# Two attention layers on one core: where the second layer keeps its scaled scores, and which engine hands a pair of score banks back

## Chip, cores and metric

One Trainium2 chip, one of its cores. The metric is the device time of one execution in microseconds (us). Engines are named as in the profile: PE (TensorE; its weight loads are listed as PEld), DVE (VectorE), ACT (ScalarE), POOL (GpSimd), SP (SyncE, which issues the transfers).

## What is computed

Two self-attention layers over 8 images of 64 x 64 positions with 64 channels, all in float32:

```python
xf = x.reshape(8, 4096, 64)
# layer 0
f = xf @ wf + bf            # 8 columns
g = xf @ wg + bg            # 8 columns
hh = xf @ wh + bh           # 64 columns
attn = softmax(einsum('bnk,bmk->bnm', g, f))
x1 = gamma0 * einsum('bnm,bmc->bnc', attn, hh) + xf
# layer 1
q = x1 @ Wq + bq;  k = x1 @ Wk + bk;  v = x1 @ Wv + bv      # 64 columns each
attn = softmax(einsum('bic,bjc->bij', q, k))
out = gamma1 * einsum('bmn,bmc->bnc', attn, v) + x1
```

In layer 1 the second product contracts over m, the index along which the rows of the softmax run: out[n] is the sum over m of attn[m, n] v[m]. So a tile with 128 values of m in its partitions and n along its columns can be used as it is, and the factor 1/(sum of row m) can be put into v[m].

## The kernel before

The program is written by hand: each engine has its own list of instructions, and semaphores hold them together. It runs through the 8 images, and for each first through layer 0 and then through layer 1 (in the code `chunk0` and `steps1`). Layer 0 is not touched by the change.

**Layer 1.** An image has T = 32 blocks of 128 queries, and each block has NCH = 4 chunks of CH = 1024 keys. One step is one chunk of one block, so a block of queries is four steps, j = 0 to 3, and an image has 128 steps. The code counts u = 0 to 7 over two blocks of queries. The steps go through four kinds of work:

- PE, `scores1` (L559 to L569): the 128 x 1024 scores of step u, into one of two pairs of PSUM banks, the pair u % 2 of `score_banks`. Queries and keys are split into float16 parts, so each half (512 columns, h = 0 and 1) takes matmuls with `k_high` and with `k_low`, two each. `s_ready` tells DVE that both halves are there.
- DVE (L1088 to L1091), called the minimum below: one instruction multiplies the 1024 scores by `neg_down` and keeps the smallest product, which is minus the largest score of each row in this chunk. It goes to `exp_bias[:, u]`. The products themselves go to a scratch tile, `scaled`, a view of `o_tr`, which nobody reads. `bias_ready` counts it.
- ACT (L811 to L819): two exponentials of 512 columns, each from one PSUM bank into `e_whole[:, u]`, with `exp_bias[:, u]` as bias and `down` as scale, and with the sum of the row in `part_sum`. `exp1_done` counts them.
- PE, `values1` (L571 to L581): seven steps later (LAG1 = 7), the slot `e_whole[:, u]` times `v_scaled[:, ..., j]` is added to `sum_banks[:, j]`. `pv1_done` counts it. `e_whole` has eight slots.

Each chunk of a row has a maximum of its own, so the row needs weights. After j = 3 DVE takes the smallest `exp_bias` of the four chunks (`neg_row1`, L1094), ACT makes four weights (`chunk_w`, L823), and in the next block of queries DVE works out from them and from `part_sum` the sum of the row and its reciprocal (`weigh_chunks`, L1061 to L1071, behind the minimum of j = 1), and then multiplies the values of the block (`weigh_values`, L1073 to L1082, behind the minimum of j = 2, written to `v_scaled`). The first `values1` of a block of queries waits for `v_scaled_ready`; PE reaches it in step j = 3 of the next block.

**Who hands a pair of banks back.** Both DVE and ACT read a bank, ACT last. So `scores1` waits, for each half by itself, for ACT's exponential of the same half two steps before:

```python
for h in range(2):
    pe.wait_ge(exp1_done, 2 * (image * STEPS1 + k) + h + 1)
```

`credit` instructions of POOL at the start (L301 to L305) put a first number on such semaphores, so that the first steps find free slots (FREE_S1, FREE_E1).

POOL is idle in most of layer 1. In blocks 8 and 9 of each image it lays out `f_stack` and `g_stack` for the image after the next (L326, L330) and adds a bias (L335). In the first two blocks of queries PE, ACT and DVE also do the projections of the same image (L415, L407) and those of a later one (L387, L397, L761).

## Time and profile before

| | |
|---|---|
| median of 3 runs | 4228.95 us (4221.15 to 4231.31) |
| the profiled execution's own time | 4228.57 us |
| its span | 4226.4 us |
| PE busy | 4030.3 us (95%) |
| DVE busy | 3271.2 us (77%) |
| ACT busy | 3191.0 us (76%) |
| POOL busy | 1953.5 us (46%) |
| granted PE clock, mean | 0.972 of full speed |
| chain that ended last | PE 84%, DVE 6%, issue 6%, ACT 3% |
| its largest lines | L480 23% (layer 0), L578 20% and L566 20% (layer 1), L466 12% (layer 0) |
| transfers | 41.88 MB, 2.9% of the 16 engines' time |

Shares are of the span. A matmul is listed from its start to its modelled end, and matmuls overlap, so the pace of PE is read from the distance between starts and not from durations. The chain of waits is followed back from the last instruction. In the timeline a bracket gives how long the engine was idle before a row, and who released it.

### The profile page before, as it was taken

Reading aid. Unit: us, or ns where it says so; the run is one execution under the profiler, and the core shown is the slowest. Engines: PE = TensorE matmul, PEld = TensorE weight load, DVE = VectorE, ACT = ScalarE, POOL = GpSimd, SP = SyncE. Lnnn points to the kernel's source line nnn. Section 1 sums busy time; section 2 is a strip of 40 time slices with the busy share of each in tenths; the row PEclk is TensorE's granted clock in tenths of the full one; section 3 lists DMA queues with packets and bytes.
Section 4 is the critical chain, followed back from the end, with each engine's and each line's share of the span. In section 5 each row is a group of like instructions: output and inputs, shape, how many; then the busy total and the mean of one; then the engine's idle time right before and its main releaser. Section 6 shows DMA issues by size and latency. Waiting matters only on the chain.

```text
span 4226.4 us, 84183 instructions
## 1 busy us (share of the span) xinstructions
PE 4030.3 (95%) x25681; PEld 1349.5 (32%) x25681; DVE 3271.2 (77%) x6298; ACT 3191.0 (76%) x5674; POOL 1953.5 (46%) x909
## 2 busy tenths in 40 slices
PE   4999999999999999999999999999999999999999
PEld 3223332233322333223332233323333233322333
DVE  3877887778877787777877788777887778877787
ACT  2466896778867788767986689776897678977788
POOL 3596106941089311992029910497105961079410
PEclk7799999999999999999999999999999999999999
DMA  1001000010000000000000000001000010000000
GB/s 33 1 1 31 1 1 11 1 31 1 1 12 11 21 1 11 1 11 21 1 12 1 18 14 1 11 1 31 1 1 12 1 31 1 1 11 3 30 1 11
DMA packets 15060, 41.88 MB, mean 10 GB/s; under 512 B 4068, under 2 KB 4068, under 8 KB 12260
## 3 DMA queue, kind: packets, MB, share of 16 engines
q1 hardware_dynamic: 14692, 36.96, 2.9%
q8 instruction: 233, 3.82, 0.4%
q14 instruction: 135, 1.11, 0.1%
HBM read 20.17 MB, written 8.39 MB: 7 GB/s over the span
## 4 chain that ended last, share of the span: by engine, by line
PE 84%; DVE 6%; issue 6%; ACT 3%; POOL 0%; SPq 0%; DVEq 0%; DMA 0%; ACTq 0%; POOLq 0%
PE sum_banks L480 23%; PE sum_banks L578 20%; PE score_banks L566 20%; PE score_banks L466 12%; PE sum_banks L502 3%; PE sum_banks L438 2%; DVE tile_max L922 1%; DVE o_tr L1089 1%; ACT e_whole L816 1%; PE score_banks L430 1%; DVE c_stack L949 1%; ACT g_tr L734 1%; PE sum_banks L415 1%; DVE k_low L969 0%; DVE x_mid L1140 0%
## 5 line engine op out<-in xcount | busy, mean ns | idle before, releaser
L816 ACT ACTIVATE e_whole<-score_banks,exp_bias,down 128x512 f32<-128x512 f32 x2048 | 1573.9, 773 | 249.8 <-DVE o_tr L1089 211.3
L922 DVE TENSOR_REDUCE tile_max<-sum_banks 128x1 f32<-128x512 f32 (+1 forms) x2128 | 1364.8, 685 | 444.0 <-PE sum_banks L438 440.5
L355 POOL TENSOR_TENSOR e_sum<-e_sum,e_whole 128x1024 f32<-128x1024 f32 x704 | 1659.5, 2357 | 83.0 <-ACT e_whole L752 31.9
L752 ACT ACTIVATE e_whole<-score_banks,no_bias,down 128x1024 f32<-128x1024 f32 x1024 | 1229.0, 1204 | 527.1 <-PE score_banks L466 516.1
L1089 DVE TENSOR_SCALAR_CACHE_REDUCE o_tr<-score_banks,neg_down 128x1024 f32<-128x1024 f32 x1024 | 1313.6, 1283 | 320.4 <-PE score_banks L566 281.4
L480 PE MATMUL sum_banks<-e_whole,proj 128*64 128x512 f32 x4096 | 1123.3, 626 | 0.0
L578 PE MATMUL sum_banks<-e_whole,v_scaled 128*64 128x512 f32 x4096 | 1066.7, 602 | 45.1 <-DVE v_scaled L1079 17.1
L566 PE MATMUL score_banks<-k_high,q_split 128*64 128x512 f16 x4096 | 810.2, 388 | 30.6 <-ACT e_whole L816 9.7
L566 PE MATMUL score_banks<-k_low,q_split 128*64 128x512 f16 x4096 | 799.2, 382 | 0.0
L438 PE MATMUL sum_banks<-f_tr,g_tr 33*128 33x512 f16 x2128 | 700.4, 402 | 19.0 <-DVE tile_max L922 14.6
L352 POOL TENSOR_TENSOR e_sum<-e_whole 128x1024 f32<-128x1024 f32 x32 | 75.4, 2357 | 1355.5 <-ACT e_whole L752 1355.5
L466 PE MATMUL score_banks<-g_tr,f_tr 34*128 34x512 f16 x2048 | 644.2, 392 | 23.7 <-ACT g_tr L734 8.7
L566 PEld LDWEIGHTS score_banks<-k_high,q_split 128*64 128x64 f16 x4096 | 228.0, 107 | 753.2 <-ACT e_whole L816 716.1
L816 ACT ACTIVATION_READ_ACCUMULATOR e_whole<-score_banks,exp_bias,down 128x1 f32 x2048 | 398.2, 194 | 0.0
L578 PEld LDWEIGHTS sum_banks<-e_whole,v_scaled 128*64 128x64 f32 x4096 | 276.7, 137 | 309.2 <-issue 145.9
L466 PEld LDWEIGHTS score_banks<-g_tr,f_tr 34*128 34x128 f16 x2048 | 120.9, 94 | 744.9 <-issue 609.6
L566 PEld LDWEIGHTS score_banks<-k_low,q_split 128*64 128x64 f16 x4096 | 242.6, 111 | 208.0 <-issue 192.6
L480 PEld LDWEIGHTS sum_banks<-e_whole,proj 128*64 128x64 f32 x4096 | 206.2, 136 | 289.2 <-ACT e_whole L752 158.0
L438 PEld LDWEIGHTS sum_banks<-f_tr,g_tr 33*128 33x128 f16 x2128 | 178.6, 94 | 182.1 <-DVE tile_max L922 102.8
L502 PE MATMUL sum_banks<-e_whole,ones_w 128*32 128x256 f32 x2048 | 164.5, 393 | 0.0
L326 POOL TENSOR_TENSOR f_stack<-fg_high,ones_h 128x512 f16<-128x512 f16 x20 | 21.3, 1077 | 258.7 <-issue 250.4
L316 POOL PARTITION_ALL_REDUCE fg_top<-fg_abs x10 | 3.7, 372 | 257.5 <-issue 257.5
(147 smaller groups left out, 1868.5 us busy)
## 6 DMA issues: line engine op xcount, KB each, us to landing
x_in<-in_x_dram SPq DMA_DIRECT2D x19, 1024.0 KB, 4.9
out_dram<-x_mid SPq DMA_DIRECT2D x32, 256.0 KB, 2.7
k_high<-k_high SPq DMA_DIRECT2D x32, 128.0 KB, 2.2
k_low<-k_low SPq DMA_DIRECT2D x32, 128.0 KB, 2.2
w<-in_L_conv_wg_dram SPq DMA_DIRECT2D x2, 2.0 KB
w<-in_L_conv_wf_dram SPq DMA_DIRECT2D x2, 2.0 KB
w<-in_L_conv_wh_dram SPq DMA_DIRECT2D x2, 16.0 KB
b<-in_L_conv_bh_dram SPq DMA_DIRECT2D x1, 32.0 KB
```

The source lines that it names most:

```text
L352: nc.gpsimd.tensor_tensor(acc, e_whole[:, 0, :], e_whole[:, 1, :], ALU.add).then_inc(e_added, 1)
L355: nc.gpsimd.tensor_tensor(acc, acc, e_whole[:, i % U0, :], ALU.add).then_inc(e_added, 1)
L438: nc.tensor.matmul(sum_banks[:, (2 + j % banks) % 4, :], g_tr[HIGH:KX, par, q * CH + blk * P:q * CH + (blk + 1) * P], f_tr[HIGH:KX, par, j ...
L466: mm = nc.tensor.matmul(score_banks[:, 2 * (i % 2) + h, :], f_tr[0:KM, par, i * P:(i + 1) * P], g_tr[0:KM, par, q * CH + h * BANK:q * CH + ...
L480: mm = nc.tensor.matmul(sum_banks[half * C:(half + 1) * C, 0, :], proj[:, par, i, GFW:PW], e_whole[:, i % U0, half * BANK:(half + 1) * BAN ...
L502: mm = nc.tensor.matmul(sum_banks[rows, 1, 0:SQ], ones_w[:, :], terms[:, c * SQ:(c + 1) * SQ], start=first, stop=final, skip_group_check=True)
L566: mm = nc.tensor.matmul(bank[c * C:(c + 1) * C, :], q_split[:, query_col(i) + c * C:query_col(i) + (c + 1) * C], k_part[:, col:col + BANK] ...
L578: mm = nc.tensor.matmul(sum_banks[half * C:(half + 1) * C, j, :], v_scaled[:, u // NCH, j, :], half_of_chunk(u, half), start=i == 0, stop= ...
L752: nc.scalar.activation(e_whole[:, i % U0, :].rearrange("p (a n) -> p a n", a=2), score_banks[:, 2 * (i % 2):2 * (i % 2) + 2, :], ACT.Exp, ...
L816: nc.scalar.activation(e_whole[:, u, h * BANK:(h + 1) * BANK], score_banks[:, 2 * (u % 2) + h, :], ACT.Exp, bias=exp_bias[:, u:u + 1], sca ...
L922: nc.vector.reduce_max(tile_max[:, blk, j:j + 1], sum_banks[:, (2 + j % banks) % 4, :], AX_X).then_inc(a_used, 1)
L1089: nc.vector.tensor_scalar(scaled[:, u % 2, :], score_banks[:, 2 * (u % 2):2 * (u % 2) + 2, :] .rearrange("p a n -> p (a n)"), neg_down[:, ...
```

## The change

In layer 1 the minimum writes its products into the slot of the probabilities, `e_whole[:, u]`, in place of the scratch tile. It therefore waits for `pv1_done` as well, which tells that the slot's last content has been used. ACT then makes one exponential of 1024 columns in place in that slot, with scale -1.0, and no longer reads PSUM; it waits for `bias_ready` alone. `part_sum` has one sum per chunk and not two. `scores1` waits for `bias_ready`, that is for DVE's minimum two steps before, once for both halves. The credit of two slots moves from `exp1_done` to `bias_ready`. `weigh_values` comes right behind `weigh_chunks` at j = 1. `down` is no longer made.

```diff
-    FREE_ST, FREE_A, FREE_E0, FREE_S1, FREE_E1 = 2, 4, U0, 4, U1
+    FREE_ST, FREE_A, FREE_E0, FREE_S1, FREE_E1 = 2, 4, U0, 2, U1
...
-            nc.gpsimd.memset(credit[:, 3:4], 0.0).then_inc(exp1_done, FREE_S1)
+            nc.gpsimd.memset(credit[:, 3:4], 0.0).then_inc(bias_ready, FREE_S1)
...
             def scores1(image, i, k, u):
+                pe.wait_ge(bias_ready, image * STEPS1 + k + 1)
                 for h in range(2):
-                    pe.wait_ge(exp1_done, 2 * (image * STEPS1 + k) + h + 1)
...
-                pe.wait_ge(exp1_done, 2 * (image * STEPS1 + t * U1 + u + 1) + FREE_S1)
+                pe.wait_ge(exp1_done, image * STEPS1 + t * U1 + u + 1)
...
-                        act.wait_ge(bias_ready, step + 1)
-                        act.wait_ge(pv1_done, step + 1)
-                        for h in range(2):
-                            nc.scalar.activation(e_whole[:, u, h * BANK:(h + 1) * BANK], score_banks[:, 2 * (u % 2) + h, :],
-                                                 ACT.Exp, bias=exp_bias[:, u:u + 1], scale=down[:, par:par + 1],
-                                                 accum_out=part_sum[:, u // NCH, u % NCH, h:h + 1]
-                                                 ).then_inc(exp1_done, 1)
+                        act.wait_ge(bias_ready, step + 1 + FREE_S1)
+                        nc.scalar.activation(e_whole[:, u, :], e_whole[:, u, :], ACT.Exp, bias=exp_bias[:, u:u + 1],
+                                             scale=-1.0, accum_out=part_sum[:, u // NCH, u % NCH:u % NCH + 1]
+                                             ).then_inc(exp1_done, 1)
...
-                    dve.wait_ge(exp1_done, 2 * (image * STEPS1 + (i + 1) * NCH) + FREE_S1)
+                    dve.wait_ge(exp1_done, image * STEPS1 + (i + 1) * NCH)
...
                         dve.wait_ge(s_ready, k + 1)
-                        nc.vector.tensor_scalar(scaled[:, u % 2, :], score_banks[:, 2 * (u % 2):2 * (u % 2) + 2, :]
+                        dve.wait_ge(pv1_done, k + 1)
+                        nc.vector.tensor_scalar(e_whole[:, u, :], score_banks[:, 2 * (u % 2):2 * (u % 2) + 2, :]
...
                             if j == 1:
                                 weigh_chunks(t * 2 + odd - 1, 1 - odd)
-                            elif j == 2:
                                 weigh_values(t * 2 + odd - 1, 1 - odd)
```

**DVE's order.** Behind the minimum of j = 1 in the loop over blocks of queries, before: `part_scr` to `norm_w` are `weigh_chunks`, `v_scaled` is `weigh_values`, ISA and REGISTER_ALU are the sequencer's own.

```order
L1065 ISA part_scr,row_sum<-part_sum,chunk_w 128x8 [waits exp1_done]
L1065 ISA row_sum 128x1
L861 ISA
L1069 RECIPROCAL inv_sum<-row_sum 128x1 [waits dve_step]
L861 REGISTER_ALU
L1070 TENSOR_SCALAR norm_w<-chunk_w,inv_sum 128x4 [waits dve_step]
L1088 REGISTER_ALU
L1089 TENSOR_SCALAR o_tr,exp_bias<-score_banks,neg_down 128x1024 [waits s_ready]
L1077 REGISTER_ALU [waits dve_step]
L1078 ISA [waits v1_biased]
L1079 ISA [waits pv1_done]
L1079 TENSOR_TENSOR v_scaled<-v,norm_w 128x256
```

and of the changed kernel, at the same place:

```order
L1058 ISA part_scr,row_sum<-part_sum,chunk_w 128x4 [waits exp1_done]
L1058 ISA row_sum 128x1
L856 ISA
L1061 RECIPROCAL inv_sum<-row_sum 128x1 [waits dve_step]
L856 REGISTER_ALU
L1062 TENSOR_SCALAR norm_w<-chunk_w,inv_sum 128x4 [waits dve_step]
L1069 REGISTER_ALU [waits dve_step]
L1070 ISA [waits v1_biased]
L1071 ISA [waits pv1_done]
L1071 TENSOR_TENSOR v_scaled<-v,norm_w 128x256
L1080 REGISTER_ALU
L1082 TENSOR_SCALAR e_whole,exp_bias<-score_banks,neg_down 128x1024 [waits pv1_done,s_ready]
```

The product for `v_scaled` now stands between the minima of j = 1 and j = 2, right behind `norm_w`, and no longer between those of j = 2 and j = 3.

**PE's order.** One step of `scores1` with the `values1` in front of it, before:

```order
L578 MATMUL sum_banks<-e_whole,v_scaled 64x512 [waits exp1_done]
L578 MATMUL sum_banks<-e_whole,v_scaled 64x512
L561 ISA
L566 MATMUL score_banks<-k_high,q_split 64x512 [waits exp1_done]
L566 MATMUL score_banks<-k_high,q_split 64x512
L566 MATMUL score_banks<-k_low,q_split 64x512 x2
L561 REGISTER_ALU
L566 MATMUL score_banks<-k_high,q_split 64x512 [waits exp1_done]
L566 MATMUL score_banks<-k_high,q_split 64x512
L566 MATMUL score_banks<-k_low,q_split 64x512 x2
```

and of the changed kernel:

```order
L576 MATMUL sum_banks<-e_whole,v_scaled 64x512 [waits exp1_done]
L576 MATMUL sum_banks<-e_whole,v_scaled 64x512
L558 REGISTER_ALU
L564 MATMUL score_banks<-k_high,q_split 64x512 [waits bias_ready]
L564 MATMUL score_banks<-k_high,q_split 64x512
L564 MATMUL score_banks<-k_low,q_split 64x512 x2
L564 MATMUL score_banks<-k_high,q_split 64x512 x2
L564 MATMUL score_banks<-k_low,q_split 64x512 x2
```

The matmuls are the same; two waits on ACT's count have become one on DVE's.

## Rows read from the trace of the kernel before

**Rows 1.** The page, part 1: busy time, share of the span, instructions.

```profile
PE 4030.3 (95%) x25681; PEld 1349.5 (32%) x25681; DVE 3271.2 (77%) x6298; ACT 3191.0 (76%) x5674; POOL 1953.5 (46%) x909
```

**Rows 2.** Windows of image 1's layer 1: length, busy per engine, granted clock.

```profile
969.00:988.00 19.00, 15.53 (x100) 5.42 (x98) 17.19 (x31) 13.91 (x37) 13.21 (x9) 1.00 0.00 1
988.00:1150.00 162.00, 159.49 (x1054) 59.28 (x1050) 134.06 (x308) 146.17 (x373) 0.00 (x0) 1.00 0.00 1
```

**Rows 3.** Waits, 988 to 1150 us: total us, times, longest.

```profile
PEld score_banks L566 <- ACT e_whole L816: 60.7, 175, 0.6
```

**Rows 4.** One line's instructions, 990 to 1151 us: ns min/median/max, first and last start.

```profile
L1079 DVE TENSOR_TENSOR v_scaled<-v,norm_w x22: 421/422/422, 994.1 to 1149.8; 128x256 f32<-128x256 f32 x22
```

**Rows 5.** Timeline, image 0, PE's two gaps in a block: start, us.

```profile
504.32 0.39 PE L566 MATMUL score_banks<-k_low,q_split 128*64 128x512 f16 x2
504.50 0.20 ACT L816 ACTIVATION_READ_ACCUMULATOR e_whole<-score_banks,exp_bias,down 128x1 f32 x1
...
504.74 0.41 PE L566 MATMUL score_banks<-k_high,q_split 128*64 128x512 f16 x2
...
506.62 0.42 DVE L1079 TENSOR_TENSOR v_scaled<-v,norm_w 128x256 f32<-128x256 f32 x1
506.71 0.38 PE L566 MATMUL score_banks<-k_low,q_split 128*64 128x512 f16 x2
...
507.17 1.08 PE L578 MATMUL sum_banks<-e_whole,v_scaled 128*64 128x512 f32 x4
...
508.94 1.03 PE L578 MATMUL sum_banks<-e_whole,v_scaled 128*64 128x512 f32 x4
...
510.66 1.03 PE L578 MATMUL sum_banks<-e_whole,v_scaled 128*64 128x512 f32 x4
```

**Rows 6.** Timeline, same block: from scores through DVE's minimum to the next minimum.

```profile
502.38 0.39 PE L566 MATMUL score_banks<-k_high,q_split 128*64 128x512 f16 x2
...
503.46 1.28 DVE L1089 TENSOR_SCALAR_CACHE_REDUCE o_tr<-score_banks,neg_down 128x1024 f32<-128x1024 f32 x1 [0.43 <-PE score_banks L566]
...
504.67 0.08 DVE L1089 DVE_READ_ACCUMULATOR o_tr<-score_banks,neg_down 128x1 f32 x1
504.67 0.16 DVE L1065 CUSTOM_DVE_ANT_1 part_scr<-part_sum,chunk_w 128x8 f32<-128x8 f32 x1
...
505.07 0.23 DVE L1070 TENSOR_SCALAR norm_w<-chunk_w,inv_sum 128x4 f32<-128x4 f32 x1
...
505.41 1.28 DVE L1089 TENSOR_SCALAR_CACHE_REDUCE o_tr<-score_banks,neg_down 128x1024 f32<-128x1024 f32 x1
...
507.13 1.28 DVE L1089 TENSOR_SCALAR_CACHE_REDUCE o_tr<-score_banks,neg_down 128x1024 f32<-128x1024 f32 x1
...
508.46 0.16 DVE L1094 TENSOR_REDUCE neg_row<-exp_bias 128x1 f32<-128x4 f32 x1
```

**Rows 7.** Groups by line and form: busy, mean ns of one, idle before.

```profile
L816 ACT ACTIVATE e_whole<-score_banks,exp_bias,down 128x512 f32<-128x512 f32 x2048 | 1573.9, 773 | 249.8 <-DVE o_tr L1089 211.3
...
L752 ACT ACTIVATE e_whole<-score_banks,no_bias,down 128x1024 f32<-128x1024 f32 x1024 | 1229.0, 1204 | 527.1 <-PE score_banks L466 516.1 <-POOL e_sum L355 9.7
...
L823 ACT ACTIVATE chunk_w<-exp_bias,neg_row 128x4 f32<-128x4 f32 x256 | 74.2, 290 | 0.0
```

**Rows 8.** Timeline of DVE in image 1, beside POOL's work in block 8.

```profile
974.35 1.27 DVE L1089 TENSOR_SCALAR_CACHE_REDUCE o_tr<-score_banks,neg_down 128x1024 f32<-128x1024 f32 x1
...
975.55 0.79 DVE L1065 CUSTOM_DVE_ANT_1 part_scr<-part_sum,chunk_w 128x8 f32<-128x8 f32 x1
...
978.46 1.13 DVE L1079 TENSOR_TENSOR v_scaled<-v,norm_w 128x256 f32<-128x256 f32 x1
```

**Rows 9.** Timeline of DVE in block 2: an operation of layer 0's between two minima.

```profile
926.99 0.69 DVE L985 TENSOR_TENSOR proj<-proj,b 128x512 f32<-128x512 f32 x1
927.83 1.28 DVE L1089 TENSOR_SCALAR_CACHE_REDUCE o_tr<-score_banks,neg_down 128x1024 f32<-128x1024 f32 x1
```

**Rows 10.** Timeline of PE in the first two blocks of image 1.

```profile
917.90 1.12 PE L397 MATMUL sum_banks<-w,x_tr 64*128 64x80 f32 x16 [0.74 <-ACT proj L761]
```

More of the change, by code:

```diff
@@ L155, in attention_pair_kernel @@
         up = sb("up", [P, 1], F32)
-        down = sb("down", [P, 2], F32)
         neg_down = sb("neg_down", [P, 2], F32)
@@ L160, in attention_pair_kernel @@
         chunk_w = sb("chunk_w", [P, 2, NCH], F32)
-        part_sum = sb("part_sum", [P, 2, NCH, 2], F32)
-        part_scr = sb("part_scr", [P, NCH, 2], F32)
+        part_sum = sb("part_sum", [P, 2, NCH], F32)
+        part_scr = sb("part_scr", [P, NCH], F32)
         row_sum1 = sb("row_sum1", [P, 2], F32)
@@ L201, in loads @@
             return image + 1 if early else image * 2
-        scaled = o_tr[:, :, :].rearrange("p (b a) n -> p b (a n)", b=2)
         g_cols = g_tr[:, :, :].rearrange("k a n -> k (a n)")
@@ L524, in chunk0 @@
                 if q == 0:
-                    pe.wait_ge(exp1_done, 2 * image * STEPS1 + FREE_S1)
+                    pe.wait_ge(bias_ready, image * STEPS1 + FREE_S1)
                     pe.wait_ge(h_biased, image + 1)
@@ L709, in image_steps @@
                 for n in range(4):
-                    pe.wait_ge(exp1_done, 2 * (image + 1) * STEPS1 - (2 if n < 2 else 0) + FREE_S1)
+                    pe.wait_ge(bias_ready, (image + 1) * STEPS1 - (1 if n < 2 else 0) + FREE_S1)
                     turn_stack(n, score_banks[:, n, :])
@@ L911, in scales @@
                 chain.link(nc.vector.tensor_scalar(up[:, :], inv_pow2[:, :], 2.0 ** HALF_TOP, None, ALU.mult))
-                nc.vector.scalar_tensor_tensor(down[:, par:par + 1], pow2[:, :], 2.0 ** (-2 * HALF_TOP), pow2[:, :],
-                                               ALU.mult, ALU.mult)
                 nc.vector.scalar_tensor_tensor(neg_down[:, par:par + 1], pow2[:, :], -2.0 ** (-2 * HALF_TOP), pow2[:, :],
@@ L1063, in weigh_chunks @@
                     dve.wait_ge(chunk_w_ready, image * T + i + 1)
-                    dve.wait_ge(exp1_done, 2 * (image * STEPS1 + (i + 1) * NCH) + FREE_S1)
+                    dve.wait_ge(exp1_done, image * STEPS1 + (i + 1) * NCH)
                     chain.link(nc.vector.tensor_tensor_reduce(
-                        out=part_scr[:, :, :], in0=part_sum[:, par, :, :],
-                        in1=chunk_w[:, par, :].unsqueeze(2).to_broadcast([P, NCH, 2]), scale=1.0, scalar=0.0,
+                        out=part_scr[:, :], in0=part_sum[:, par, :], in1=chunk_w[:, par, :], scale=1.0, scalar=0.0,
                         op0=ALU.mult, op1=ALU.add, accum_out=row_sum1[:, par:par + 1]))
@@ L1092, in steps1 @@
                         if j == NCH - 1:
-                            dve.wait_ge(bias_ready, k + 1)
+                            dve.wait_ge(bias_ready, k + 1 + FREE_S1)
                             nc.vector.tensor_reduce(neg_row1[:, odd:odd + 1], exp_bias[:, odd * NCH:(odd + 1) * NCH],
```

## The prediction

> **What bounds the kernel now.** I read the page's busy shares first: PE is busy for 95% of the span, DVE 77%, ACT 76% [rows 1]. But PE's durations overlap, so this does not say that PE is at its pace, and it mixes two layers. The change touches layer 1 alone, so I took windows of it. In the quiet part of an image, 988 to 1150 us, DVE is busy 134.06 of 162 us and ACT 146.17 (90%), at the full granted clock, 2.4 GHz [rows 2]. Then one line by its starts: `v_scaled` is made once per block of queries, and its 22 starts lie (1149.8 - 994.1) / 21 = 7.41 us apart [rows 4]. What PE could do is read where it runs without a gap: two `values1` starts with one step between them lie 510.66 - 508.94 = 1.72 us apart [rows 5], so four steps are 6.88 us. PE loses 7.41 - 6.88 = 0.53 us in each block of queries.
>
> The timeline shows where. First gap: a pair of matmuls normally follows the last by 1.72 / 8 = 0.215 us, but between 504.32 and 504.74 lie 0.42 us, and the later one starts 0.04 us behind ACT's readout (504.50 + 0.20) [rows 5]: 0.20 us lost, because the bank's half is held by the exponential. The waits agree: ACT is named 175 times in 162 us as releaser of the scores' weight loads [rows 3]; most of these are short and hidden, since the load comes ahead of its matmul. Second gap: `values1` starts at 507.17, 0.46 us behind the last scores pair at 506.71, and `v_scaled` ended at 506.62 + 0.42 = 507.04 [rows 5]: 0.25 us lost, waiting for DVE's product, which stands behind the minimum of j = 2. The rest, 0.08 us, is slower restarting behind the two. So layer 1 is bound by PE with two gaps, one made by ACT, one by the order on DVE. The change aims at both.
>
> **The change part by part.** All times below count from T, the start of the scores of step j = 1.
>
> *The banks come back from DVE.* DVE's minimum starts 503.46 - 502.38 = 1.08 us behind the start of its scores, the next operation follows 1.21 us after it (504.67), and its result is out after 1.29 us (504.67 + 0.08) [rows 6]. PE then follows 0.04 us later. In a plain step the pair is free at 1.08 + 1.29 + 0.04 = 2.41 us, and PE wants it after two steps, 3.44 us. First gap gone, with 1.03 us to spare.
>
> *The weights' work comes together.* Behind the minimum of j = 1 DVE now does all of it. Its length W: from `part_scr` to the end of `norm_w`, 505.07 + 0.23 - 504.67 = 0.63 us; `v_scaled` to the next minimum, 507.13 - 506.62 = 0.51 us [rows 5, 6]; and between them a wait for `norm_w` and two more instructions of the sequencer, which no row of before shows in this place. At least they cost nothing; at most, three times the 0.11 us between `norm_w`'s end (505.30) and the next minimum (505.41), where one such instruction stands [rows 6]: 0.33 us. I take that upper value, since the three come one after the other with nothing to hide them, so W = 1.47 us (1.14 at least). The minimum of j = 2 then ends for PE at T + 1.08 + 1.21 + W + 1.29 + 0.04 = T + 3.62 + W = T + 5.09. PE wants that pair after three steps, T + 5.16. It fits by 0.07 us, up to W = 1.54. This is the tight place of the change. Behind it, the whole load of DVE per block is 4 x 1.21 + 1.47 + 0.28 for `neg_row1` (508.46 + 0.16 - 507.13 - 1.21 [rows 6]) = 6.59 us, under 6.88. `v_scaled` is ready at T + 1.08 + 1.21 + 1.47 - 0.09 = T + 3.67, and PE wants it behind the scores of j = 3, at T + 3.44 + 0.86 = T + 4.30: second gap gone.
>
> *ACT's exponential.* Two of 773 ns become one of 1024 columns from SBUF, which no row shows. Lower bound: `chunk_w`, also from SBUF and with one pointer operand, takes 290 ns at 4 columns, and a column costs (1204 - 773) / 512 = 0.84 ns [rows 7], so 290 + 859 = 1.15 us. Upper: 1.204 us as L752, with the 0.20 us readout wholly behind it, 1.40 us [rows 5, 7]. I take the upper one; nothing hangs on it: 4 x 1.40 + 0.29 = 5.89 us per block, under 6.88. `values1` needs it seven steps later. `chunk_w` matters more, since `weigh_chunks` waits for it in front of the minimum of j = 2: by the same walk the exponentials of j = 2 and 3 end at T + 6.49 and T + 7.89 and the weights at T + 8.18, and DVE asks at T + 6.88 + 2.29 = T + 9.17. One microsecond to spare.
>
> The Trainium skill (VectorE: DVE Perf Modes, section "The TRN2 errata — SBUF-src ops pay a fixed extra latency per instruction") speaks against this step: ACT pays 224 fixed cycles from SBUF and 172 from PSUM. An estimate from that page is 0.04 us per exponential, 44 us over 1024 of them if ACT set the pace, and nothing in the sum as long as it does not; no row of before has the same exponential from both memories.
>
> *The minimum's new wait.* It waits for `pv1_done` of the slot's last use. PE has done that product one step before it sends the scores that the same minimum waits for, so it costs nothing. The dropped `down`, the halved `part_sum` and the one wait fewer per step on PE: nothing, off the path or hidden behind matmuls.
>
> *The sum, per image.* An image has 32 blocks of queries; the first two are filled with other work.
> - 30 blocks by 0.53 us by 8 images: 127 us.
> - In some four blocks of an image DVE has one more operation in front of the minimum of j = 1. L985 takes 927.83 - 926.99 = 0.84 us there [rows 9]. From the minimum of j = 0 the walk is 1.08 + 1.21 + 0.84 + 1.21 + 1.47 + 1.33 = 7.14 us against 6.88, so 0.26 us late; others are shorter. I take 0.2: 4 x 0.2 x 8 = 6 us given back (0 to 8).
> - Blocks 8 and 9, beside POOL: DVE's small operations grow, `part_scr` to 0.79 and `v_scaled` to 1.13 us [rows 8], and in 19 us PE is idle for 3.47 [rows 2]. These operations come all the same, so most of the stall stays. Between nothing and 1.1 us more per image; I take 0.6, 5 us in all.
> - The first two blocks: one of PE's waits there is for ACT's copy of the projections (917.90, 0.74 us) [rows 10], and ACT is less loaded; their other waits I leave as they are. Between 0 and 2.5 us; I take 0.9 by the one row, 7 us in all.
> - The end of the layer is PE's own chain of products and transposes: nothing. Layer 0: nothing.
>
> 127 - 6 + 5 + 7 = 133 us. The profiled execution took 4228.6 us itself (the median of the runs is 4228.95, the same), so 4096 us.
>
> **The rivals.**
>
> *DVE's bundle is too long.* The block then takes 1.72 + 3.62 + W = 5.34 + W. At W = 1.84, 0.1 us more for each of the three sequencer instructions and a late start, it takes 7.18, 0.30 more than in the forecast: 240 blocks by 0.30 = 72 us, so 4168 us; 4115 to 4190 for what lies around it. For it: only 0.07 us to spare. Against: W is already at its upper bound.
>
> *The release is not what holds PE.* If `chunk_w` came late, DVE would stand in front of the minimum of j = 2 and PE behind it, and the chain would again run over ACT. It needs more than 1 us of delay over two exponentials, so about 1.9 us each instead of 1.40. The old pace is reached at (7.41 - 0.29) / 4 = 1.78 us per exponential. Then 4229 less the start, 4222 to 4230. Against: 1.204 us from PSUM. The rule on SBUF sources would make 1.44.
>
> *Slower: the minimum pays for its new place.* It now writes into the tile that ACT reads and writes and PE streams from, where before it had a scratch tile to itself. With d more per minimum DVE's load is 6.59 + 4d; it passes the old 7.41 us at d = 0.21. At d = 0.3 a block takes 7.79, 0.38 more than before: 240 by 0.38 = 91 us, so 4320 us. For it: small DVE operations grow fourfold beside POOL. Against: the minimum itself takes 1.27 us even there [rows 8], and L816 has written to that tile while PE read it all along.
>
> **How the numbers follow.** The forecast has 0.76 (4065 to 4115: the low end adds 1.1 and 2.5 us per image for the two bounded terms and leaves the 6 us out, 4072, and a little for what I don't see), the too long bundle 0.15, no change 0.05, slower 0.04. The range 4065 to 4145 leaves out the far half of the second case and the last two. About 13 us (0.3%) is what can be told from no change. Faster 0.91, same 0.05, slower 0.04.
>
> **What would show it.** The starts of `v_scaled` 6.88 us apart in the quiet part; ACT gone as releaser of the scores' weight loads; `values1` of j = 0 without a wait for `v_scaled`; one exponential of 1.15 to 1.2 us per step and ACT's busy time in layer 1 down by a quarter; DVE's minimum still at 1.28 us; between `norm_w` and `v_scaled` at most 0.33 us. I am wrong if the blocks stay above 7.0 us: with DVE named in front of the scores of j = 0 it was the bundle, with ACT in front of `part_scr` it was the weights, with the minimum above 1.4 us it was the new place.

## The result, and the profile after

The changed kernel takes 4096.85 us (median of 4 runs, 4095.08 to 4101.33); the kernel before, on the same chip, 4225.3 us (4221.15 to 4231.31). The ratio is 0.9697, with a 95% interval of 0.9681 to 0.9712: 3% faster, 128 us. The forecast was 4096.0 us. The profiled execution has a span of 4094.2 us and a mean granted clock of 0.973, against 4226.4 us and 0.972 before.

The page of the changed kernel, part 1, which answers to [rows 1], and from its part 5 the two groups of layer 1 that replace the minimum and the exponentials of [rows 7] (busy us and mean ns of one, then idle time before and its releaser):

```profile
PE 3912.5 (96%) x25681; PEld 1450.7 (35%) x25681; DVE 3265.9 (80%) x6288; ACT 2789.5 (68%) x3626; POOL 1951.2 (48%) x909
...
L812 ACT ACTIVATE e_whole<-e_whole,exp_bias 128x1024 f32<-128x1024 f32 x1024 | 1176.1, 1149 | 518.4 <-DVE e_whole L1082 500.8
...
L1082 DVE TENSOR_SCALAR_CACHE_REDUCE e_whole<-score_banks,neg_down 128x1024 f32<-128x1024 f32 x1024 | 1292.8, 1281 | 132.0 <-PE score_banks L564 122.3
```

DVE's busy time is the same as before, ACT's is 402 us less. The minimum takes 1.281 us (1.283 before), so its new place costs it nothing. The exponential takes 1.149 us, exactly the lower bound of the prediction, which left the readout of the sum out; where two exponentials follow each other in the timeline, the second starts 1.20 us behind the first (500.57 and 501.77 in image 0).

Windows of image 1's layer 1, with the columns of [rows 2]: the first blocks of queries up to block 7 (905 to 949), blocks 8 and 9 beside POOL (949 to 968), and the quiet part:

```profile
905.00:949.00 44.00, 44.00 (x310) 23.62 (x308) 40.77 (x96) 32.12 (x59) 0.38 (x2) 1.00 0.01 1
949.00:968.00 19.00, 15.71 (x96) 6.22 (x94) 17.28 (x29) 10.05 (x19) 12.90 (x9) 0.91 0.01 2
968.00:1116.00 148.00, 148.00 (x1036) 64.63 (x1034) 129.47 (x302) 109.61 (x193) 0.00 (x0) 1.00 0.00 1
```

In the first and the last of them PE is busy all the time. ACT was busy 90% of its window before and is now busy 109.61 / 148 = 74%. Beside POOL the picture is another one: PE is idle for 3.29 of 19 us, as before (3.47), and the mean granted clock is 0.91 there.

The line that gave the pace in [rows 4], here from 968 to 1116 us:

```profile
L1071 DVE TENSOR_TENSOR v_scaled<-v,norm_w x22: 424/426/427, 970.5 to 1115.0; 128x256 f32<-128x256 f32 x22
```

(1115.0 - 970.5) / 21 = 6.88 us per block of queries, PE's own pace. The waits of the same stretch (total us, times, longest), for comparison with [rows 3]:

```profile
ACT e_whole L812 <- DVE e_whole L1082: 37.7, 44, 1.3
PEld score_banks L564 <- issue: 35.0, 119, 0.3
PEld score_banks L564 <- DVE e_whole L1082: 15.8, 42, 0.5
```

ACT, named 175 times before as releaser of the scores' weight loads, is gone from that place. DVE is named 42 times for at most 0.5 us, all of it hidden, since PE itself is never idle. The chain that ended last shows the same thing at the place where [rows 5] showed two gaps (start us, us, group). It now runs on PE alone, and a step takes 1.72 us, two rows of 0.86:

```profile
500.22 0.86 PE sum_banks L576 x4
501.08 0.86 PE score_banks L564 x8
501.94 0.86 PE sum_banks L576 x4
502.80 0.86 PE score_banks L564 x8
503.66 0.86 PE sum_banks L576 x4
```

Last, the tight place of the change: the timeline of DVE from `part_scr` to the next minimum, in two blocks that follow each other (image 0).

```profile
504.92 0.16 DVE L1058 CUSTOM_DVE_ANT_0 part_scr<-part_sum,chunk_w 128x4 f32<-128x4 f32 x1
...
505.31 0.23 DVE L1062 TENSOR_SCALAR norm_w<-chunk_w,inv_sum 128x4 f32<-128x4 f32 x1
505.94 0.42 DVE L1071 TENSOR_TENSOR v_scaled<-v,norm_w 128x256 f32<-128x256 f32 x1 [0.39 <-DVE norm_w L1062]
506.28 1.28 DVE L1082 TENSOR_SCALAR_CACHE_REDUCE e_whole<-score_banks,neg_down 128x1024 f32<-128x1024 f32 x1
...
511.80 0.16 DVE L1058 CUSTOM_DVE_ANT_0 part_scr<-part_sum,chunk_w 128x4 f32<-128x4 f32 x1
...
512.20 0.23 DVE L1062 TENSOR_SCALAR norm_w<-chunk_w,inv_sum 128x4 f32<-128x4 f32 x1
512.68 0.43 DVE L1071 TENSOR_TENSOR v_scaled<-v,norm_w 128x256 f32<-128x256 f32 x1 [0.25 <-DVE norm_w L1062]
513.02 1.28 DVE L1082 TENSOR_SCALAR_CACHE_REDUCE e_whole<-score_banks,neg_down 128x1024 f32<-128x1024 f32 x1
```

The length W is 506.28 - 504.92 = 1.36 us in one block and 513.02 - 511.80 = 1.22 us in the next, 1.29 on average, where the prediction had 1.47.

**Where the 128 us come from.** From the first to the last scores of an image, layer 1 took 250.5 us before and takes 234.0 now (means of the 8 images); the rest of an image, layer 0, takes 259.5 and 259.3. So all of it is layer 1: 16.5 x 8 = 132 us, which is the difference of the two profiled spans; the medians differ by 128. By the starts of DVE's minima, summed over the 8 images:

| blocks of queries of an image | before | after | difference | forecast |
|---|---|---|---|---|
| 0 and 1 (with layer 0's leftovers) | 188.0 | 177.8 | -10.2 | -7 |
| 2 to 7 (some with one more operation) | 359.3 | 330.6 | -28.7 | -19 (25 less 6) |
| 8 to 10 (beside POOL) | 214.4 | 210.2 | -4.2 | -18 (13 and 5) |
| 11 to 30 (quiet) | 1186.7 | 1101.8 | -84.9 | -85 |

The last 4 us are in block 31 and behind it, where 4 were forecast. The quiet blocks came out to the microsecond. The three small terms did not: two gains were larger than forecast and one far smaller, and they cancelled.

### The profile page after: what moved, and what is told of

It is laid out like the page before. It is cut to its first block, busy times and chain, and to the rows that moved or that the text cites. A ratio compares the mean times of both kernels' runs of the same rounds, so it can differ in the third digit from the quotient of the medians.

```text
span 4094.2 us, 80429 instructions
## 1 busy us (share of the span) xinstructions
PE 3912.5 (96%) x25681; PEld 1450.7 (35%) x25681; DVE 3265.9 (80%) x6288; ACT 2789.5 (68%) x3626; POOL 1951.2 (48%) x909
## 4 chain that ended last, share of the span: by engine, by line
PE 84%; DVE 8%; issue 5%; ACT 2%; DVEq 0%; SPq 0%; POOL 0%; DMA 0%; ACTq 0%; POOLq 0%
PE sum_banks L478 24%; PE score_banks L564 20%; PE sum_banks L576 20%; PE score_banks L464 12%; PE sum_banks L500 3%; PE sum_banks L436 2%; DVE tile_max L915 2%; DVE e_whole L1082 1%; DVE part_scr L1058 1%; DVE c_stack L942 1%; ACT g_tr L732 1%; PE score_banks L428 1%; PE sum_banks L413 1%; DVE k_low L962 1%; DVE x_abs L896 0%
## 5 line engine op out<-in xcount | busy, mean ns | idle before, releaser
L750 ACT ACTIVATE e_whole<-score_banks,no_bias,down 128x1024 f32<-128x1024 f32 x1024 | 1228.8, 1204 | 530.4 <-PE score_banks L464 515.7
L812 ACT ACTIVATE e_whole<-e_whole,exp_bias 128x1024 f32<-128x1024 f32 x1024 | 1176.1, 1149 | 518.4 <-DVE e_whole L1082 500.8
L1082 DVE TENSOR_SCALAR_CACHE_REDUCE e_whole<-score_banks,neg_down 128x1024 f32<-128x1024 f32 x1024 | 1292.8, 1281 | 132.0 <-PE score_banks L564 122.3
L576 PE MATMUL sum_banks<-e_whole,v_scaled 128*64 128x512 f32 x4096 | 1056.1, 596 | 40.9 <-DVE v_scaled L1071 29.7
L564 PEld LDWEIGHTS score_banks<-k_high,q_split 128*64 128x64 f16 x4096 | 247.5, 110 | 445.9 <-issue 176.5
L576 PEld LDWEIGHTS sum_banks<-e_whole,v_scaled 128*64 128x64 f32 x4096 | 301.8, 137 | 233.9 <-issue 43.5
L812 ACT ACTIVATION_READ_ACCUMULATOR e_whole<-e_whole,exp_bias 128x1 f32 x1024 | 191.0, 187 | 0.0
L1071 DVE TENSOR_TENSOR v_scaled<-v,norm_w 128x256 f32<-128x256 f32 x256 | 115.2, 450 | 63.1 <-DVE norm_w L1062 61.1
```

The lines of the kernel that those rows point to most:

```text
L564: mm = nc.tensor.matmul(bank[c * C:(c + 1) * C, :], q_split[:, query_col(i) + c * C:query_col(i) + (c + 1) * C], k_part[:, col:col + BANK] ...
L576: mm = nc.tensor.matmul(sum_banks[half * C:(half + 1) * C, j, :], v_scaled[:, u // NCH, j, :], half_of_chunk(u, half), start=i == 0, stop= ...
L750: nc.scalar.activation(e_whole[:, i % U0, :].rearrange("p (a n) -> p a n", a=2), score_banks[:, 2 * (i % 2):2 * (i % 2) + 2, :], ACT.Exp, ...
L812: nc.scalar.activation(e_whole[:, u, :], e_whole[:, u, :], ACT.Exp, bias=exp_bias[:, u:u + 1], scale=-1.0, accum_out=part_sum[:, u // NCH, ...
L1071: nc.vector.tensor_tensor(v_scaled[:, par, :, :], v1[:, i, :].unsqueeze(1).to_broadcast([P, NCH, C]), norm_w[:, par, :].unsqueeze(2).to_br ...
L1082: nc.vector.tensor_scalar(e_whole[:, u, :], score_banks[:, 2 * (u % 2):2 * (u % 2) + 2, :] .rearrange("p a n -> p (a n)"), neg_down[:, par ...
```

## The experiments

Ten kernels, each timed against the kernel before on its own chip. A ratio is to that kernel. "Theory" is, in experiments 1 to 5, the walk of the prediction with its tight place, and in 7 to 10 a rule for what POOL does to DVE.

**1. The order alone.** The kernel before, with `weigh_values` moved to j = 1 and nothing else.

```diff
                             if j == 1:
                                 weigh_chunks(t * 2 + odd - 1, 1 - odd)
-                            elif j == 2:
                                 weigh_values(t * 2 + odd - 1, 1 - odd)
```

> The kernel before with only the order of DVE changed: the values are weighed right behind the weights at j = 1. Theory: the two parts of the change need each other. As long as ACT hands the banks back, the pair of j = 0 is free only behind DVE's bundle, the minimum of j = 2 and two exponentials; the bundle in front of it grows from 0.74 to about 1.3 us, so a block of queries takes longer than 7.41 us by about that, 7.8 to 7.9 us: slower than before, 4290 to 4360 us. Rival (the two gaps are independent and add up): the wait for v_scaled goes, 0.25 us per block, 4165 us.

Measured: 4314.91 us, ratio 1.021 (1.0193 to 1.0227). The starts of `v_scaled` in the quiet part:

```profile
L1079 DVE TENSOR_TENSOR v_scaled<-v,norm_w x21: 424/425/428, 1000.4 to 1158.4; 128x256 f32<-128x256 f32 x21
```

(1158.4 - 1000.4) / 20 = 7.90 us per block, 0.49 more than before. This half of the change is a loss of 2% by itself. The bundle delays the minimum of j = 2, and as long as the pair comes back by way of ACT the delay runs on through two exponentials to PE: from 1000 to 1160 us the scores' weight loads wait for ACT for up to 1.2 us, where the longest such wait was 0.6 [rows 3]. That the parts of the change simply add up has fallen.

**2. The release alone.** The changed kernel, with `weigh_values` back at j = 2. It keeps the minimum's new place and the one exponential too.

```diff
                                 weigh_chunks(t * 2 + odd - 1, 1 - odd)
+                            elif j == 2:
                                 weigh_values(t * 2 + odd - 1, 1 - odd)
```

> The changed kernel with the product for v_scaled put back behind the minimum of j = 2. Theory: PE, no longer held by the banks, now comes to the first product of a block of queries at T + 4.30 us, and v_scaled is there at T + 4.79 us, so the one gap that is left grows to about 0.49 us per block: blocks of 7.3 to 7.4 us, 4195 to 4220 us. Rival (the gap keeps the 0.25 us that it had before): 4160 us.

Measured: 4171.18 us, ratio 0.9867 (0.9851 to 0.9884), between the rival and the theory's range.

```profile
L1071 DVE TENSOR_TENSOR v_scaled<-v,norm_w x18: 419/420/423, 1002.9 to 1125.1; 128x256 f32<-128x256 f32 x18
```

(1125.1 - 1002.9) / 17 = 7.19 us per block: the first gap is gone and the second has stayed, 0.31 us. The timeline tells why it is less than I had it. In one block:

```profile
1001.14 0.16 DVE L1058 CUSTOM_DVE_ANT_0 part_scr<-part_sum,chunk_w 128x4 f32<-128x4 f32 x1
...
1001.73 1.28 DVE L1082 TENSOR_SCALAR_CACHE_REDUCE e_whole<-score_banks,neg_down 128x1024 f32<-128x1024 f32 x1
...
1002.94 0.42 DVE L1071 TENSOR_TENSOR v_scaled<-v,norm_w 128x256 f32<-128x256 f32 x1
...
1003.42 1.08 PE L576 MATMUL sum_banks<-e_whole,v_scaled 128*64 128x512 f32 x4
```

From `part_scr` to the minimum it is 1001.73 - 1001.14 = 0.59 us here, and 505.41 - 504.67 = 0.74 in [rows 6]. Those 0.74 us had held a wait for PE's scores, which is not a cost of the operations: the scores' last pair ended at 504.98 + 0.38 = 505.36, and the minimum came at 505.41. PE's `values1` starts 0.06 us behind the end of `v_scaled` (1003.36).

**3. The banks come back from ACT.** The changed kernel with everything in place (minimum into the slot, one exponential, the new order), but `scores1` waits for the exponential.

```diff
-                pe.wait_ge(bias_ready, image * STEPS1 + k + 1)
+                pe.wait_ge(exp1_done, image * STEPS1 + k + 1)
```

(and the credit of two slots moves back to `exp1_done` with it).

> The changed kernel (products in the slot of the probabilities, one exponential in place, weights and values together), but the banks are handed back by ACT's exponential as before. Theory: it is the hand-over that pays. The pair of j = 0 comes back at T + 1.08 + 1.21 + 1.3 + 1.29 + 0.04 + 1.15 + 0.15 = T + 6.2 us, so a block takes 7.9 us: slower than before, 4330 to 4390 us. Rival (the shorter exponential is what pays): near the changed kernel, below 4150 us.

Measured: 4331.73 us, ratio 1.0248 (1.0228 to 1.0267); the blocks take 8.01 and 7.86 us in turn. From the waits of the whole run, and the starts of `v_scaled` in the quiet part:

```profile
PEld score_banks L564 <- ACT e_whole L812: 844.4, 965, 2.6
```

```profile
L1071 DVE TENSOR_TENSOR v_scaled<-v,norm_w x22: 424/425/426, 1001.5 to 1168.3; 128x256 f32<-128x256 f32 x22
```

(1168.3 - 1001.5) / 21 = 7.94 us. The nearest kernel is that of experiment 1, with the same order and hand-over but ACT's old work, and it has 7.90. So one exponential fewer per step, and no PSUM read on ACT, bring nothing by themselves in this order. This kernel is 5.7% slower than the changed one, though ACT is as light in it (2795.6 us busy). The hand-over is what pays.

**4 and 5. How much room the bundle has.** The changed kernel with one or two more products of 256 columns in front of `v_scaled`, written to a tile that nobody reads (N = 2 or 1).

```diff
+                    for n in range(N):
+                        nc.vector.tensor_tensor(v_more[:, n, :, :],
+                                                v1[:, i, :].unsqueeze(1).to_broadcast([P, NCH, C]),
+                                                norm_w[:, par, :].unsqueeze(2).to_broadcast([P, NCH, C]), ALU.mult)
```

Two more:

> The changed kernel with two more products of the size of v_scaled's in DVE's bundle at j = 1, written to a tile that nobody reads. The bundle W grows from 1.29 us (mean of 1.36 and 1.22) to about 2.1 us. Theory (the path through the bundle and the minimum of j = 2 sets a block, 5.34 + W): 7.4 us per block in the quiet part, 4097 + 240 x 0.55 = 4230 us. Rival (DVE's load alone counts, 4 x 1.21 + 0.28 + W = 7.2 us): 4170 us. Second rival (there is more room than worked out): 4100 us.

One more, after the result with two:

> The changed kernel with one more product in DVE's bundle, W = 1.63 us on average (1.56 and 1.70). Theory (the path through the bundle and the minimum of j = 2, 5.34 + W by the rows of before, 5.43 + W by the run with two more): blocks of 6.97 to 7.06 us in the quiet part, 4115 to 4145 us. Rival (DVE's load alone, 4 x 1.21 + 0.28 + 1.63 = 6.75 us, under PE's 6.88): 4097 us, no change.

Measured: with two 4220.16 us, ratio 0.9987 (0.9977 to 0.9996); with one 4138.32 us, ratio 0.9799 (0.9784 to 0.9814). The blocks, first with two and then with one:

```profile
L1076 DVE TENSOR_TENSOR v_scaled<-v,norm_w x19: 417/419/420, 999.8 to 1133.0; 128x256 f32<-128x256 f32 x19
```

```profile
L1076 DVE TENSOR_TENSOR v_scaled<-v,norm_w x18: 416/418/421, 1003.5 to 1123.4; 128x256 f32<-128x256 f32 x18
```

(1133.0 - 999.8) / 18 = 7.40 us and (1123.4 - 1003.5) / 17 = 7.05 us. With two, W is 2.04 and 1.90 us in turn, 1.97 on average, so a block takes 5.43 us more than W; with one, W is 1.70 and 1.56, 1.63 on average, and it is 5.42. The prediction's walk gave 5.34. DVE's load in a block is 6.41 us now (4 x 1.21 + 1.29 + 0.28); two products make about 7.1 and one 6.75, which is under PE's 6.88 and would have cost nothing if load were what counts. It cost 41 us. The path over the minimum of j = 2 sets the block as soon as W is over 6.88 - 5.43 = 1.45 us; the changed kernel's 1.29 has 0.16 us to spare, and the longer of its two values, 1.36, has 0.09.

**6. What ACT's exponential costs.** The changed kernel with the scale -1 from a column of SBUF in place of a constant, so that the exponential has two pointer operands as L752 of layer 0 has.

```diff
-                                             scale=-1.0, accum_out=part_sum[:, u // NCH, u % NCH:u % NCH + 1]
+                                             scale=minus[:, 0:1], accum_out=part_sum[:, u // NCH, u % NCH:u % NCH + 1]
```

> The changed kernel with the scale of ACT's exponential in place read from a column of SBUF, as the exponential of before had it, and not given in the instruction. It tells what the memory costs: with two pointer operands 1024 columns from PSUM take 1.204 us in layer 0. If a source in SBUF costs a fixed 0.04 us more, and a pointer 0.09 us, this exponential takes 1.24 us; if the memory costs nothing, it takes 1.204 us and the pointer 0.05 us. Either way ACT is far from setting the pace, so the time stays at 4097 us.

Measured: 4091.53 us (2 runs), ratio 0.9688 (0.9671 to 0.9706), so no change of the time. Its group on the page, part 5:

```profile
L814 ACT ACTIVATE e_whole<-e_whole,exp_bias,minus 128x1024 f32<-128x1024 f32 x1024 | 1266.6, 1237 | 443.6 <-DVE e_whole L1084 438.7
```

1237 - 1149 = 88 ns is the price of the pointer operand. The nearest instruction from PSUM is L752 with 1204 ns [rows 7], also with two pointers; it makes no sum of the row, so SBUF as the source costs 33 ns if the sum costs the exponential itself nothing. Another pair gives 41 ns: L769 in the changed kernel, with one pointer, 1024 columns from PSUM, another function and no sum, takes 1108 ns against 1149. The prediction's estimate from the Trainium skill (VectorE: DVE Perf Modes, "The TRN2 errata — SBUF-src ops pay a fixed extra latency per instruction") was 0.04 us for this, and the trace agrees with 0.033 and 0.041. ACT's busy time rose by 71 us (2860.2 against 2789.5) and the run did not get longer, which is the other thing it shows: ACT's length does not matter at this size. That it is even 5 us shorter lies in blocks 8 to 10 (203.8 against 210.2 us over the 8 images), where the granted clock fell in two images, and in six in the changed kernel (see experiment 7).

**7. The stall beside POOL.** The table above left one question: why blocks 8 to 10 gained 4 us where 18 were forecast. In block 9 of image 1 the changed kernel's timeline reads:

```profile
957.32 4.58 POOL L333 TENSOR_TENSOR proj<-proj,b 128x2048 f32<-128x2048 f32 x1
```

```profile
958.75 3.17 DVE L1058 CUSTOM_DVE_ANT_0 part_scr<-part_sum,chunk_w 128x4 f32<-128x4 f32 x1
...
962.91 1.72 PE L576 MATMUL sum_banks<-e_whole,v_scaled 128*64 128x512 f32 x4 [1.97 <-DVE v_scaled L1071]
964.41 0.65 PE L564 MATMUL score_banks<-k_high,q_split 128*64 128x512 f16 x2
...
966.12 1.28 PE L576 MATMUL sum_banks<-e_whole,v_scaled 128*64 128x512 f32 x4
967.23 0.39 PE L564 MATMUL score_banks<-k_high,q_split 128*64 128x512 f16 x2
...
968.09 1.03 PE L576 MATMUL sum_banks<-e_whole,v_scaled 128*64 128x512 f32 x4
```

`part_scr`, four columns wide, takes 3.17 us in place of 0.16. It ends at 961.92; POOL's bias addition ends at 961.90. PE stands for 1.97 us. Behind that its matmuls are slower for two steps, the scores' pair 0.65 in place of 0.39 us, at half the clock, as the windows of the changed kernel show, in the columns of [rows 2] (0.50, which is 1.2 GHz):

```profile
963.20:966.60 3.40, 3.40 (x14) 1.17 (x12) 2.44 (x6) 2.51 (x5) 0.00 (x0) 0.50 0.02 5
```

Before it fell PE had stood still for the 1.97 us. `values1` starts at 962.91, 966.12 and 968.09, so the two steps take 5.18 us in place of 3.44, and 1.74 us more are lost. A long `part_scr` stands beside this addition in each of the 8 images, and the clock fell behind it in six of them, 20.5 us at half the clock in all. It had fallen in six before the change too (23.9 us), though not in image 1, which [rows 2] shows. PE was idle in blocks 8 to 10 for 25.4 us before, over the 8 images, and is for 28.7 now: the gaps of the quiet blocks went, and the stalls beside POOL grew. The cure to try is a POOL instruction in pieces:

```diff
+                for n in range(PIECES):
+                    h = proj[:, par, n * (T // PIECES):(n + 1) * (T // PIECES), GFW:PW]
+                    nc.gpsimd.tensor_tensor(h, h, b0[:, GFW:PW].unsqueeze(1).to_broadcast([P, T // PIECES, C]), ALU.add
+                                            ).then_inc(h_biased, 1)
```

With PIECES = 8:

> The changed kernel with POOL's bias for the projections (one instruction of 4.6 us beside blocks 8 and 9 of an image) cut into eight of 4 blocks each; nothing else. Theory: DVE's operations with two inputs in SBUF wait for the end of the POOL instruction that is running, so part_scr, which took 3.17 to 4.15 us there in each of the 8 images, now waits for 0.6 us at most, and the clock falls less often behind it: 2 to 3.5 us per image, 4070 to 4082 us. Rival (POOL and DVE share a bandwidth, so the length of a POOL instruction doesn't matter): 4097 us, with part_scr as long as before.

Measured: 4074.7 us, ratio 0.9643 (0.963 to 0.9656). The same place, and all of `part_scr` in the run:

```profile
953.35 5.76 POOL L335 TENSOR_TENSOR proj<-proj,b 128x256 f32<-128x256 f32 x8
```

```profile
954.78 0.71 DVE L1060 CUSTOM_DVE_ANT_0 part_scr<-part_sum,chunk_w 128x4 f32<-128x4 f32 x1
```

```profile
L1060 DVE CUSTOM_DVE_ANT_0 part_scr<-part_sum,chunk_w x256: 156/158/1050, 403.2 to 4059.8; 128x4 f32<-128x4 f32 x128
```

The longest `part_scr` falls from 4.15 to 1.05 us, and blocks 8 to 10 from 210.2 to 185.7 us over the 8 images, 24.5 us, which covers the whole gain. PE is idle there for 13.0 us in place of 28.7, and the clock does not fall in any of them. That small operations wait for the end of POOL's running instruction holds.

**8. All of POOL's instructions in pieces.** If that is the whole rule, shorter is always better. The eight instructions for `f_stack` and `g_stack` too, each in four:

```diff
+                    cuts = [slice(n * (T // CUTS), (n + 1) * (T // CUTS)) for n in range(CUTS)]
...
+                        for rows in cuts:
+                            src = part[:, rows, 1, :].unsqueeze(2).to_broadcast([P, T // CUTS, 2, CK])
+                            dst = f_stack[:, rows, col:col + 2 * CK].rearrange("p t (r c) -> p t r c", r=2)
+                            nc.gpsimd.tensor_tensor(dst, src, one, ALU.mult).then_inc(f_stacked, 1)
```

> As the run before it, and the eight instructions with which POOL lays out the stacks (1.0 us each) are cut in four each as well. Theory: the waits of part_scr, norm_w and v_scaled for these (0.6, 0.5 and 0.8 us above their usual time) shrink too, by up to 1 us per image; against it stands what more instructions cost POOL, which is free there: 4062 to 4078 us, not slower than the run before it. Rival: the finer instructions only let DVE collide more often: the same as the run before it or slower.

Measured: 4142.86 us, ratio 0.981 (0.9797 to 0.9824), 68 us slower than with the bias alone in pieces. A clear miss. Image 1:

```profile
966.61 9.01 DVE L1064 CUSTOM_DVE_ANT_0 part_scr<-part_sum,chunk_w 128x4 f32<-128x4 f32 x1
```

```profile
967.26 2.90 POOL L333 TENSOR_TENSOR g_stack<-fg_low,ones_h 128x128 f16<-128x128 f16 x8
970.11 5.48 POOL L339 TENSOR_TENSOR proj<-proj,b 128x256 f32<-128x256 f32 x8
```

`part_scr` began 0.07 us behind the start of one of POOL's short instructions and did not get its turn between it and any of the 17 that followed without a gap. It ended at 975.61, 0.01 us behind the last (975.60). It came out so in each of the 8 images (9.01 us in seven of them and 9.36 in one), and blocks 8 to 10 took 250.8 us. The clock has a share in it: late in the stall and behind it, it was at half for 6.8 or 10.2 us in each image, 68.3 us in all, where it did not fall with the bias alone in pieces. So the rule is wider than I had it: the small operation does not always get in at the next boundary.

**9. Is it the length of the pieces?** The bias in 16 pieces, the rest as in the changed kernel.

> The changed kernel with POOL's bias in sixteen pieces of about 0.3 us, back to back, and the stack instructions whole. It asks what shut part_scr out for 9 us in the run with everything cut, beside seventeen short POOL instructions. Theory A (pieces under some 0.4 us leave DVE no moment to get in): part_scr is shut out for up to 5 us again, and the time is 4085 to 4110 us. Theory B (it was a matter of phase between the two engines and not of the length): part_scr waits for one piece, 4068 to 4078 us.

Measured: 4075.81 us, ratio 0.964 (0.9625 to 0.9655), the same as with eight.

```profile
L1060 DVE CUSTOM_DVE_ANT_0 part_scr<-part_sum,chunk_w x256: 156/159/973, 404.6 to 4055.2; 128x4 f32<-128x4 f32 x128
```

No `part_scr` is over 0.97 us, so shorter pieces do not by themselves shut DVE out. What decided it in experiment 8 stays open. A plain rule of phase does not fit: in experiment 7 `part_scr` began 0.05 us behind the start of a piece of the bias (image 1, 954.78) and got its turn at the end of that piece, and in experiment 8 it was passed over when it began 0.06 or 0.07 us behind the start of one of `f_stack`.

**10. POOL's work behind the minima.** Without knowing the rule one can keep the two apart. Eight pieces of bias again, and each of POOL's portions waits for the minimum of a step j = 2, 3 or 0, so that none is running where the bundle of j = 1 stands.

```diff
+    SLOTS = (34, 35, 36, 38, 39, 40, 42, 43, 44, 46, 47, 48)
...
+            def behind(image, slot):
+                if image is not None:
+                    pool.wait_ge(bias_ready, image * STEPS1 + SLOTS[slot] + 1 + FREE_S1)
```

> The changed kernel with POOL's bias in eight pieces, and POOL held to DVE's pace in blocks 8 to 12 of an image: each of the eight stack instructions (1.0 us) and each pair of bias pieces (2 x 0.6 us) waits for the end of a minimum of j = 2, 3 or 0, behind which DVE has another minimum of 1.28 us, and none starts behind that of j = 1, where the bundle stands. Theory: the minimum, which reads PSUM, doesn't wait for POOL, and part_scr, norm_w and v_scaled don't meet it any more, so they take 0.16, 0.23 and 0.43 us everywhere: up to 2.5 us per image under the run with the bias in eight alone (4075 us), 4053 to 4066 us. Rival (the stall in these blocks is made by the operations of layer 0's that DVE has there, not by POOL): 4075 us.

Measured: 4057.31 us, ratio 0.9595 (0.9582 to 0.9608). All of `part_scr`:

```profile
L1072 DVE CUSTOM_DVE_ANT_0 part_scr<-part_sum,chunk_w x256: 156/158/397, 403.4 to 4041.9; 128x4 f32<-128x4 f32 x128
```

`norm_w` is never over 0.23 and `v_scaled` never over 0.43 us. Blocks 8 to 10 take 166.6 us, 6.9 each, which is PE's pace; PE is never idle there, and the clock does not fall. The gain over the changed kernel, 40 us, is the 43.6 us of these blocks within 4. This kernel beats both: 4.05% faster than before, where the change alone is 3.03% faster.

## Why the prediction was right, and where it was not

**The main term was right, by its own mechanism.** 0.53 us per block, from 7.41 to 6.88, was forecast and measured to the second digit, and both gaps closed. The two halves of the change need each other, which the prediction's walk contained without saying so: alone they make +0.49 us (order) and -0.22 us (release), together -0.53. Experiment 3 shows that it is the hand-over by DVE and not the lighter ACT.

**ACT was right.** The exponential was bounded by 1.15 us without the readout of its sum and 1.40 us with it, and taken at the upper end. It takes 1.149 and, with the readout, 1.20 to the next; experiment 6 shows that nothing hangs on it.

**The tight place was read too long, by a wait taken for a cost.** The step "`v_scaled` to the next minimum, 507.13 - 506.62 = 0.51 us" held DVE's wait for PE's scores; without it the distance is 0.34 us (505.94 to 506.28). The 0.11 us behind `norm_w`, of which three were taken, were the same wait: in experiment 2 the minimum starts 0.04 us before `norm_w` ends (1001.73 and 1001.54 + 0.23). So the 0.33 us "at most" for the way from `norm_w` to `v_scaled` were right in size by luck, and they were no upper bound: `norm_w` ends at 505.54 and `v_scaled` starts at 505.94, 0.40 us later, and in the next block 0.25 us later (512.43 to 512.68). Together W is 1.29 and not 1.47, and the room is 1.45 (experiments 4 and 5) and not 1.54. So "it fits by 0.07 us" should have read 0.16. The rival of the bundle that is too long named the right mechanism at the right slope: it expected 7.18 us at W = 1.84, and the measured line gives 7.27.

**"I take 0.2: 6 us given back" was wrong.** Blocks 2 to 7 gained 28.7 us, more than the full 25.4. They take 330.6 / 48 = 6.89 us now and had taken 359.3 / 48 = 7.49, more than the quiet ones, which I had not looked at. The walk put 0.84 us more in front of the minimum of j = 1, with a W of 1.47. In these blocks W is shorter than anywhere in the quiet part, 923.58 - 922.58 = 1.00 us:

```profile
922.58 0.16 DVE L1058 CUSTOM_DVE_ANT_0 part_scr<-part_sum,chunk_w 128x4 f32<-128x4 f32 x1
...
922.98 0.23 DVE L1062 TENSOR_SCALAR norm_w<-chunk_w,inv_sum 128x4 f32<-128x4 f32 x1
923.24 0.43 DVE L1071 TENSOR_TENSOR v_scaled<-v,norm_w 128x256 f32<-128x256 f32 x1
923.58 1.28 DVE L1082 TENSOR_SCALAR_CACHE_REDUCE e_whole<-score_banks,neg_down 128x1024 f32<-128x1024 f32 x1
```

`v_scaled` starts 0.03 us behind the end of `norm_w` and not 0.25 or 0.40. With W = 1.00 the walk is 7.14 - 0.47 = 6.67 us against 6.88, so nothing is late, and PE was busy for 44.00 of 44.00 us there. The program writes blocks 0 to 9 out one by one and runs blocks 10 to 31 as a loop of the engine (`dve.Fori(5, T // 2)`), and the longer distance begins with block 10 in each of the 8 images. That what the sequencer does in the loop is the reason is likely and not tested.

**The term beside POOL was wrong in its sign.** "Most of the stall stays. Between nothing and 1.1 us more per image; I take 0.6": these three blocks gained 4.2 us over the 8 images, where 12.7 by the pace and 5 by this term were in the sum, so 13.5 us are missing. The lower bound, "nothing", left out a loss without giving a reason. The row that it went by, `part_scr` at 0.79 us [rows 8], was a meeting with one of POOL's short instructions (1.03 us), and what such a meeting costs depends on when it comes and on which of POOL's instructions it meets. All of `part_scr` in the kernel before, and in the changed one:

```profile
L1065 DVE CUSTOM_DVE_ANT_1 part_scr<-part_sum,chunk_w x256: 159/162/2424, 404.7 to 4212.9; 128x8 f32<-128x8 f32 x128
```

```profile
L1058 DVE CUSTOM_DVE_ANT_0 part_scr<-part_sum,chunk_w x256: 156/158/4152, 405.3 to 4080.8; 128x4 f32<-128x4 f32 x128
```

The longest was 2.4 us before and is 4.2 now, since at the new pace `part_scr` meets the long bias addition in every image, where it had met it in four of the 8. Over all 256 of them `part_scr` took 9 us more than its usual time before and takes 31 us more now. The maximum of 2424 ns was there to be read before the change.

The Trainium skill (SBUF — State Buffer, "Who interferes with whom") has the rule: DVE with two inputs in SBUF and a GpSimd instruction that reads SBUF exclude each other for a whole instruction. The ends at 961.92 and 961.90 agree, and so does the minimum, with its one tensor from PSUM, which keeps its 1.27 us there [rows 8]. By that rule an estimate for the price of a meeting is anything up to the length of POOL's instruction, 4.58 us, and not 0.79. Experiment 8 goes beyond the rule: 9.01 us beside POOL instructions of 0.40 and 0.72 us, so there the wait did not end with the instruction that was running.

**The sum was right partly by luck.** Blocks 2 to 7 gave 9 us more than forecast, the first two 3 us more, and the blocks beside POOL 14 us less. With only the last of these errors the forecast would have been 14 us too low, still inside 4065 to 4145. The starting point has a share too: the forecast took its 133 us from 4228.6 us, and the kernel before has 4225.3 in the runs beside the changed one, so by the medians the gain is 128 us. The agreement to 1 us is that of a large term which was right and of small ones which cancelled.

## What to carry to other kernels

When several engines read a buffer in turn, move the release to the one that can copy it out first, and do it before or together with any reordering on that engine: here the reordering without it cost 2%. A distance between two starts is a cost only if the engine was not waiting in it: before it goes into a tight sum, look for the releaser of the second; and read it in the part of the program that it is for, since the same operations took 1.00 us in blocks written out and 1.29 in the loop. Where two engines exclude each other for whole instructions, read the longest duration of the small operations in all of the kernel and not the one in a single row, and place the long work by a semaphore where the critical bundle does not run.

## What the runs showed of the hardware

- `part_scr`, four columns from SBUF, ends 0.02 us behind the end of the POOL instruction that runs beside it (961.92 and 961.90). The minimum, which reads PSUM, takes its 1.27 us even there [rows 8].
- In experiment 8 a DVE operation was passed over while POOL ran one instruction to its end and 17 more without a gap, 9.01 us (18 more and 9.36 us in one of the 8 images); beside 8 or 16 pieces of the bias alone it waited for at most about one microsecond. The cause is open.
- PE's stall of 1.97 us was paid for almost twice, since 1.74 us more went in the slower matmuls behind it, at a granted clock of 0.50 for 3.4 us. Whether it falls is not settled by the stall: the same stall beside POOL was followed by it in six images of 8 before, in six after and in two of experiment 6, with 25.4, 28.7 and 27.8 us of idle PE in these blocks.
- `v_scaled`, a DVE operation that waits for DVE's own result with instructions of the sequencer between, starts 0.03 us after the end of `norm_w` in most blocks that the program writes out, and 0.40 or 0.25 us after it, in turn from block to block, in the loop.
- A pointer operand costs ACT 88 ns, and SBUF in place of PSUM as the source 33 or 41 ns (two pairs of instructions, each of which differs in the sum of the row too), at 1024 columns.
